# Queries' step: TensorE's output product behind the projection, VectorE's last sum behind the low half of O

## The reference

```
x = x + L0(gn(x))                         # 3x3 convolution with rotated kernels, gated
t = tokens(gn(x))                         # (B, 4096, 256)
q = (relu(t Wq + bq) + 1e-6) / scale      # k the same way, v plain
q = q^3 * |q| / |q^3|                     # k too
z = 1 / (q . sum(k) + 1e-6)
out = (q @ (k^T v)) * z + depthwise5x5(v)
x = x + out @ Wproj + bproj
```

## Time and profile before

| what | us |
|---|---|
| median of 3 runs | 3930.86 |
| range of the runs | 3926.9 to 3932.67 |
| the profiled execution | 3932.86 |
| its span, first to last instruction | 3930.8 |
| PE busy | 3542.5 |
| DVE busy | 2972.1 |
| ACT busy | 2711.0 |
| POOL busy | 1426.4 |

### The profile page before, as it was taken

One profiled execution on the slowest core, in us unless ns is written; L12 is line 12 of the kernel. 1 busy time (PEld: TensorE's weight loads), 2 busy tenths in 40 slices (PEclk: granted clock), 3 DMA queues, 4 the chain that ended last, 5 costly groups with the idle time before them and its releaser, 6 DMA issues.

```text
span 3930.8 us, 96093 instructions
## 1 busy us (share of the span) xinstructions
PE 3542.5 (90%) x27980; PEld 2861.4 (73%) x27980; DVE 2972.1 (76%) x8235; ACT 2711.0 (69%) x7348; POOL 1426.4 (36%) x1318
## 2 busy tenths in 40 slices
PE   0569999999999999989999998999999899999797
PEld 0238777777877778777777877777787777778686
DVE  6767887868778786877868788786878878585756
ACT  2247776776777667676766767777677767677675
POOL 4632442514334252443514244351424425140302
PEclk9889999999999999999999999999999999999999
DMA  4672534536354462635436263443636354260302
GB/s 156 205 238 66 169 105 138 169 90 189 110 154 120 129 177 79 189 107 150 134 110 192 73 186 117 141 141 112 179 92 181 102 148 127 83 181 21 103 17 76
DMA packets 560048, 516.44 MB, mean 131 GB/s; under 512 B 97600, under 2 KB 491968, under 8 KB 559552
## 3 DMA queue, kind: packets, MB, share of 16 engines
q1 hardware_dynamic: 555200, 508.99, 43.9%
q10 hardware_dynamic: 4352, 1.57, 0.2%
HBM read 351.06 MB, written 134.22 MB: 123 GB/s over the span
## 4 chain that ended last, share of the span: by engine, by line
PE 42%; DVE 26%; issue 14%; ACT 13%; DMA 2%; DVEq 2%; SPq 1%; ACTq 0%; POOL 0%; POOLq 0%
PE F L1518 9%; PE VAB L1518 7%; PE F L1557 6%; ACT K L1295 6%; PE T L1529 5%; PE VAB L1557 5%; DVE F L975 4%; DVE XR L1064 3%; DVE XR L1057 3%; DVE XHL L969 3%; DVE XR L1046 2%; ACT K L1301 2%; PE PP L1608 2%; DVE ST L962 1%; DVE RATIO L989 1%
## 5 line engine op out<-in xcount | busy, mean ns | idle before, releaser
L1518 PE MATMUL F<-WQ,XHL 128*128 128x256 f16 x6144 | 822.7, 275 | 27.3 <-ACT V L1335 19.0
L650 POOL TENSOR_TENSOR XR<-XR,V 128x512 f32<-128x512 f32 x256 | 326.0, 1274 | 1038.9 <-DVE XR L1046 1038.9
L1518 PEld LDWEIGHTS F<-WQ,XHL 128*128 128x128 f16 (+1 forms) x6144 | 603.4, 99 | 105.6 <-issue 33.6
L1295 ACT ACTIVATE K<-F,SCAL 128x256 f32<-128x256 f32 x1024 | 476.3, 471 | 292.3 <-DVE F L975 279.7
L1504 PE MATMUL SM<-SL,BD 128*128 128x512 f16 x2688 | 634.9, 385 | 0.0
L634 POOL TENSOR_TENSOR SL<-PL,SL 128x1122 f16<-128x1122 f32 x112 | 260.1, 2322 | 1031.8 <-DVE SL L947 1031.8
L1301 ACT ACTIVATE K<-K,SCAL 128x256 f32<-128x256 f32 x1024 | 514.0, 510 | 160.9 <-DVE K L981 160.8
L981 DVE TENSOR_TENSOR K<-K,F 128x512 f32<-128x512 f32 x512 | 351.6, 687 | 282.0 <-ACT K L1295 184.0
L975 DVE TENSOR_TENSOR F<-F,FL 128x512 f32<-128x512 f32 x512 | 353.9, 691 | 154.4 <-PE F L1520 148.3
L1504 PEld LDWEIGHTS SM<-SL,BD 128*128 128x128 f16 x2688 | 261.0, 97 | 284.1
L1608 PE MATMUL PP<-XR,WP 128*128 128x256 f16 x3072 | 388.9, 278 | 67.8 <-DVE XR L1064 67.8
(11 more groups left out here) (194 smaller groups left out, 6954.6 us busy)
## 6 DMA issues: line engine op xcount, KB each, us to landing
XR<-xr SPq DMA_DIRECT2D x132, 512.0 KB, 5.3
U<-x SPq DMA_DIRECT2D x256, 256.0 KB, 3.8
XR<-x SPq DMA_DIRECT2D x256, 256.0 KB, 4.1
out<-XR SPq DMA_DIRECT2D x256, 256.0 KB, 3.8
PL<-xp SPq DMA_DIRECT2D x112, 561.0 KB, 3.8
RX<-xr SPq DMA_DIRECT2D x118, 512.0 KB, 4.0
x<-RX SPq DMA_DIRECT2D x448, 128.0 KB, 2.1
BD<-RX SPq DMA_DIRECT2D x240, 96.0 KB, 2.2
```

The lines of the kernel that those rows point to most:

```text
L650: g_.tensor_tensor(o, o, fm, ALU.add).then_inc(o_rdy, 2)
L1295: a.activation(K2[:, p, ts], F[p][:, ts], ACT.Square, scale=inv_a, accum_out=S2[:, 2 * p + t:2 * p + t + 1]).then_inc(f_sq, 1)
L1518: t_.matmul(o, XHL[:, xa, h, at], WQ[:, wa, h, c0:c0 + C], start=(k == 0), stop=False)
```

## The change

In TensorE's step, output moves from between attention and transpose_o to between project and transpose_q. In VectorE's step, finish moves from behind the quotients to between low_out and floor_max. Nothing is added or taken away, and no wait is changed.

```diff
@@ VectorE, step_q
                     quotients(b, u - 1, p)
-                if live(p - 4):
-                    finish(b, u - 2, p)
                 if conv and 0 <= k < 2 * GROUPS:
                     result_stats(b + 2, k)
...
                 if live(p - 3):
                     low_out(b, u - 2 + p, 1 - p)
+                if live(p - 4):
+                    finish(b, u - 2, p)
                 if live(p) or keys:
                     floor_max(n, p)
@@ TensorE, step_q
                 if live(p - 2):
                     attention(b, u - 1, p)
-                if live(p - 4):
-                    output(b, u - 2, p)
                 if live(p - 3):
                     transpose_o(b, u - 2 + p, 1 - p)
                 if live(p):
...
                     project(b, u, p, F, 0)
                 elif nxt and u == NU:
                     keys(b + 1, 0, p)
+                if live(p - 4):
+                    output(b, u - 2, p)
                 if live(p - 1):
                     transpose_q(b, u - 1 + p, 1 - p)
```

## The result

Beside runs of the kernel before on the same chip (median 3928.88 us of 4, 3917.77 to 3932.67) the changed kernel takes 4054.01 us (median of 4, 4048.37 to 4061.59): ratio 1.0332, 95% interval 1.0309 to 1.0354, so 125 us slower. The prediction was 4052 in a range of 4012 to 4084. The profiled execution took 4048.37 us, its span is 4046.3, 115.5 us more than the span before. The traces are less far apart than the medians, since the execution profiled here is the shortest of its four, and the one profiled before (3932.86) was longer than all four runs beside it.

What follows compares the result with a forecast made beforehand. VectorE and ACT were taken to bound steps from step 8. Batches 0 to 13 at 8.18 us each (114.5), batch 14 8.6 and the tail -1.2 summed to +121.9 us, forecast 4052 us, range 4012 to 4084.

Steps and rivals of the forecast that it cites:

- What bounds the steps: Queries' stage from step 8: VectorE and ACT set the pace, 15.05 us for two steps against TensorE's 14.56.
- The cast is held by POOL's add, so finish had been covered: VectorE's cast L969 ends 0.28 us behind POOL's add; finish ahead filled that gap, moved it costs 0.66 us a step.
- 12 x 0.66 - 0.40 = 7.52 us a batch: Steps 6 to 17: finish costs 0.66 us each, less slack of 0.29 and 0.11 us behind steps 6 and 15.
- steps 4 and 5, put at nothing: Steps 4 and 5 of the queries' stage: no cast, TensorE sets the pace, so the change costs nothing.
- The planes' 0.6 us to spare: SP's planes load, behind the later store, lands by 1176.6 at the latest; ACT reads at 1177.2, 0.6 us to spare.
- A: Main case: the held cast had covered finish, so moving it costs +121.9 us in all, 4052 us; chance 0.76.
- rival C: SP's later store delays the planes' load, 0.4 us a pair lost, +34 us, 4086 us; chance 0.07.
- End of a stage: Step 19: output of tile 15 waits for finish of tile 14, now behind low_out; next batch 0.66 us later.
- +1.25 an end: Upper bound at a stage's end: 1.25 us beyond 0.66 if longer idle makes more matmuls run at the slow pace.
- The tail: Batch 15's end: outputs leave the chain, one finish with its landing enters; -1.2 us, bounds -2.6 and 0.
- Batch 15's steps, put at nothing: Batch 15 has no casts, so the change costs nothing in its steps.
- Output behind the projection costs nothing: TensorE: twelve matmuls change place with transposes and projection, nothing added; next attention comes no sooner; price nothing.

Runs made afterwards that it cites:

- planes first: Changed kernel with SP issuing the planes' load ahead of the store instead of behind it: 4046.09 us, ratio 1.0306 to the kernel before.
- half add in the kernel before: Control: kernel before the change with POOL's add (L650) over only half of each tile's channels: 3890.8 us, ratio 0.9921.
- half add: Changed kernel with POOL's add (L650) over only half of each tile's channels: 3994.97 us, ratio 1.0186 to the kernel before.
- both: Changed kernel with POOL's add halved and the planes' load ahead of the store: 3949.52 us, ratio 1.007 to the kernel before.

## Why the prediction was right, and where it was not

**What bounds the steps.** Right, but for a wait of 0.12 us for the convolution in step 9, in 13 of 14 batches. VectorE and ACT set steps 6 and later through the ring floor, squares, cube, quotients, floor; TensorE's idle time doesn't help. Half of POOL's add takes 59 us from the changed kernel, with TensorE's work unchanged.

**The cast is held by POOL's add, so finish had been covered.** Shown, not only argued: ahead of the cast finish costs nothing (ratio 1.0001), directly behind it 96 us, and the cast's end follows the add's end at 0.28 to 0.29 us whether the add takes 1.27 or 0.72 us. This holds for all 180 casts that overlap an add in the trace of before. The Trainium skill, "SBUF — State Buffer", section "Who interferes with whom", says that whichever of the two engines starts first keeps the shared ports for the length of its instruction. The held casts agree with that: the sooner they start behind the start of the add, the longer they are drawn, up to 1.04 us, against 0.41 to 0.43 for those outside an add. In no run did this cast begin ahead of the add, but it did begin ahead of POOL's other sum, L641, about 20 times in each trace without being held itself. Timeline of the changed kernel, where the cast is 0.01 us ahead:

```profile
255.87 0.43 DVE L969 CAST XHL<-U 128x512 f16<-128x512 f32 x1 [0.16 <-ACT U L1286]
255.88 1.42 POOL L641 TENSOR_TENSOR XHL<-U,XHL 128x512 f16<-128x512 f32 x1 [3.51 <-DVE XHL L969]
```

Here the cast keeps its 0.43 us, and L641 is the one that is drawn longer, 1.42 us where it takes 1.15 to 1.17 alone. In all these cases L641 ends 1.01 to 1.02 us behind the end of the cast. So the other side of the rule is seen too, and the trace agrees with it.

**12 x 0.66 - 0.40 = 7.52 us a batch.** Without the late planes (the kernel with the planes first) a stage of batches 0 to 12 takes 127.6 to 127.7 us against 120.15: 7.5 us. The terms one by one, from the floors: step 7 grew by 0.38 (predicted 0.37), step 16 by 0.55 (0.55), the others by 0.64 to 0.66. Batch 14: 8.2 against 7.9. Its steps 4 and 5, put at nothing, grew by 0.22 us each (5.30 to 5.52): without a convolution VectorE and ACT set these steps too.

**The planes' 0.6 us to spare.** This step failed, though with a small price. A was to hold without rival C. In fact ACT waited 34 times for the planes, and that cost 12 us in the stages (1796.6 against 1784.8 with the planes first). The order of SP's queue was read rightly. Mis-sized were two terms. The larger is the landing: I bounded it by the longest of one window, 5.1 us, where the longest in the whole trace of before is 5.7, and in that window of the changed kernel it reached 6.6 us (7.0 in the whole trace), with two stores and two loads issued just ahead. The smaller is the issue: the load goes out 3.7 us behind the end of finish, where I had counted 3.2. A and C were not alternatives: both mechanisms were in the result, C at 12 instead of 34 us.

**End of a stage.** Right in the mechanism; its size is not resolved. The end of the same batch as in the earlier trace rows, changed kernel:

```profile
1243.78 0.69 DVE L975 TENSOR_TENSOR F<-F,FL 128x512 f32<-128x512 f32 x1
...
1248.85 0.75 DVE L1064 SCALAR_TENSOR_TENSOR XR<-T,SCAL,XR 128x512 f16<-128x512 f32 x1
1249.52 0.74 DVE L1057 SCALAR_TENSOR_TENSOR XR<-PP,SCAL,XR 128x512 f32<-128x512 f32 x1
...
1250.41 2.72 PE L1608 MATMUL PP<-XR,WP 128*128 128x256 f16 x12 [3.40 <-DVE XR L1057]
...
1259.04 0.70 DVE L975 TENSOR_TENSOR F<-F,FL 128x512 f32<-128x512 f32 x1 [1.67 <-PE F L1520]
```

Output waits for L1057, 1.56 us behind low_out's start instead of 0.80, and 6.63 us behind the last floor instead of 5.88: +0.75, with 0.66 predicted. Yet from there to the next floor it took 8.63 instead of 9.69 us, and over 15 ends the time between stages fell by 7.1 us where +9.9 was predicted. The same stretch, from output to the next floor, by windows (engines' busy us, then TensorE's granted clock, DMA share, GB/s), before:

```profile
1215.10:1224.79 9.69, 7.99 (x44) 5.61 (x45) 5.34 (x10) 4.42 (x10) 5.29 (x9) 0.68 0.23 63
```

and after:

```profile
1250.41:1259.04 8.63, 6.29 (x44) 4.76 (x45) 4.05 (x9) 4.22 (x10) 4.84 (x9) 0.85 0.24 69
```

The same number of matmuls ran at a mean granted clock of 0.85 instead of 0.68. Of the levels 1.2 and 2.4 GHz the lower lasted longer before. I had a bound for the price of a longer idle only on the upper side (+1.25 an end); the lower side, a stretch that comes out faster, was missing. The order alone doesn't decide this. With the order of before at the ends, the time between the stages is 1656.9, 1634.7 and 1639.4 us in three kernels (before, finish directly ahead of the cast, half add in the kernel before), of which 113, 75 and 75 us were at the lower clock. With the order of the changed kernel it is 1649.8, 1657.6, 1651.2 and 1647.3 us in four (changed, planes first, half add, both). The means are 8 us apart, which would fit the 9.9 predicted, but one order alone scatters by 22 us. The trace of before happened to have the slowest ends of its order, and what decides the clock from one end to the next stays open.

**The tail.** Predicted -1.2 us; from the last floor to the last instruction it is 17.7 instead of 19.2 us. Batch 15's steps, put at nothing, took 1.5 us more, so the whole batch stands at nothing. About 0.7 of that comes in its first steps and is there with finish directly ahead of the cast too. The rest is in the four steps that VectorE and ACT had set at 5.30 us, which now take 5.52 like the others.

**Output behind the projection costs nothing.** Right for the whole change, for a reason that the prediction gave only in part. It is free because finish moves too. Alone it costs 129 us, nearly as much as the other half (143).

The total of 4054 against 4052 is therefore closer than its parts, and that is luck. By the traces the difference is 115.5 us where 121.9 was the sum. The 12 us of late planes are missing in the sum. Too much in it are 17 us between the stages and 2 us at the start, which differ between traces of one order as well; the steps are met within 1 us, and batch 15 makes up the remaining 1 us. By the medians the difference is 125 us: there the 12 us that are missing for the planes and the 10 us put down for the ends, whose size no run resolves, may stand against each other.

## What to carry to other kernels

Look at where an instruction ends, not only at how long it is: a cast whose end keeps a fixed distance to another engine's end is being held, and what is queued ahead of it costs nothing as long as it is done before the hold ends and doesn't itself wait, while the same instruction behind it costs its full length. Put there what the loop is waiting for: the order with floor_max ahead of the cast gave 0.8%, and finish taken from there lost 2.4% directly behind the cast and 3.7% behind low_out. When a change moves a producer and its consumer, try each half alone before calling either of them free. Before reading a difference of some 10 us between two traces, look how far apart traces of one order are in that part.

## What the hardware showed that was not expected

A held cast doesn't wait to the recorded end of POOL's instruction and then run its full length. The 128x512 cast takes 0.41 us free and ends 0.28 us behind the add, so its own work begins some 0.13 us ahead of the add's recorded end. For the 128x1122 cast it is the same: 0.75 us free, and held by L641 (1166.32, 1.16 us; with the half add) it ends at 1168.08, 0.60 us behind that, so 0.15 us ahead. Estimating a held instruction as the other's end plus its full length would be too long by that. The other way round it is alike: L641 takes 1.15 us alone and, held by a cast, ends 1.01 us behind the cast's end, so 0.14 us ahead.

The time for a load to land is no constant of the load: in the same window the planes took up to 5.1 us before, up to 6.6 us behind two stores and two loads, and 4.2 us at most with the planes first in the queue.
